# Output product of an attention kernel as seven block products instead of eight

## The chip, the cores and the metric

The kernel runs on one core of one Trainium2 chip. The metric is its device time in microseconds: median 2259.83 us of three runs (2258.32 to 2260.1).

## What is computed

Three steps on 4 sequences of 512 tokens, each 1024 wide, all in fp32: a gated feed-forward step, latent attention with 32 heads, and the feed-forward step again, each added to x. The change is in the attention:

```python
q = rms_norm(x @ wq_a.T, q_norm_w) @ wq_b.T            # 32 heads: 128 plain, 64 rotated columns
kv_up = rms_norm(kv_c, kv_norm_w) @ wkv_b.T            # keys and values from 128 latents
scores = (q_nope . k_nope + q_pe . k_pe) * scale       # causal
probs = softmax(scores)
out = (probs . v).reshape(b, s, 32 * 128)
x = x + out @ wo.T                                     # [512, 4096] x [4096, 1024] per sequence
```

## The kernel before

An fp32 number is kept as two fp32r parts, high and low, and a product is three matmuls: high x high, high x low, low x high (`three`, L781; `products` issues them, the matmul is L777).

Attention treats two of the four sequences at a time (a pair, p = 0 and 1) and two heads at a time (a group, g = 0 to 15). A group has four slots, k = 0 to 3; a slot is half of one sequence for both heads. Slots of even k take the first half and have few keys ("even slots"), those of odd k the second half ("odd slots"). In slot k PE does, by an order written out in `slot` (L1191): the four score tiles of the slot (`scores`), the transposes of the four probability tiles of the slot before (`turn_probs`), the values of the slot before (`values`), the output product of the slot before that (`output`), and "fills", which prepare queries and weights and are spread over the slots by the table `FILLS`: q0 to q3 and pe0, pe1 (nine matmuls 512 columns wide each), and in pair 0 also m0 to m3 (value weights times output weights, one true fp32 matmul 512 wide) and w0, w1.

The values of a slot are [latent 128] x [2 heads x 256 rows]. The output product multiplies them with `w_out` (2 heads x 1024 columns): four outputs of 128 rows x 512 columns, j = 0 to 3, each six matmuls (two heads x three), which is eight block products of three matmuls. The bank of output j is one of two (`bank_y`), so PE waits for the addition of output j-2 to `xacc`.

- ACT reads PSUM and writes high parts (`hi`, L1303): `turned` for transposes, `valued` for values, `read_fill`; it also does the exponentials (`exps`, L1579).
- DVE does masks and maxima (`maxima`), the low parts (`lo`, L1692: `pt_split`, `o_split`, fills), the scaling of probabilities (`norms`, L2029) and the additions (`y_add`, L2041).
- POOL does the rotation of the rotated query half, five links of 512 columns (`rotate`, L2278 to L2286), twice a group, after a swap by DMA, and the low part of the rotated weights (`split_wpe`, L2257).
- SP issues the swaps and stacks of the rotation, loads of weights, and in pair 0 stores `w_out` (`keep_wo`); in pair 1 ACT issues its reload (`out_weights`).

Each engine goes through its list in order. `settle` is a semaphore increment between waits.

## Time and profile before

| | |
|---|---|
| median of the runs | 2259.83 us |
| span of the profiled execution | 2257.3 us |
| PE busy | 2213.3 us, 98% |
| DVE busy | 1594.8 us, 71% |
| ACT busy | 968.0 us, 43% |
| POOL busy | 576.2 us, 26% |
| steady group in pair 0 (4 slots) | 63.10 us |
| steady group in pair 1 (4 slots) | 57.57 us |

No time of the profiled execution beyond its span is shown; the median lies 2.5 us above the span. The two attention stages repeat exactly from group to group, so one group is read closely and multiplied.

### The profile page before, as it was taken

What the parts mean: (1) busy time and instruction counts of PE and PEld (TensorE: products, weight loads), DVE (VectorE), ACT (ScalarE), POOL (GpSimd) and SP (SyncE); (2) the same over time, 40 slices, a digit from 0 to 9 for tenths busy, and PEclk for the clock granted to TensorE, in tenths of its full rate; (3) what the DMA queues carried; (4) which work ended last, traced back from release to release, by engine and by line L of the source; (5) the groups of instructions that cost most, each with busy time, mean ns of one, the idle gap of its engine ahead of it and who ended that gap; (6) DMA issues with size and microseconds to landing.
All of it is one profiled execution on the core that took longest, in us unless ns stands there. A gap on an engine that the chain in (4) does not pass through costs nothing.

```text
span 2257.3 us, 39455 instructions
## 1 busy us (share of the span) xinstructions
PE 2213.3 (98%) x11932; PEld 1871.3 (83%) x11932; DVE 1594.8 (71%) x3663; ACT 968.0 (43%) x2441; POOL 576.2 (26%) x642
## 2 busy tenths in 40 slices
PE   8989999999999999999999999999999999999998
PEld 7978888888888888887788988888888888888887
DVE  7656667776676766777787666766777766666777
ACT  6543444443444443443465534334344443334344
POOL 5312222122221222212144332222222222222212
PEclk9999999999999999999999999999999999999999
DMA  4023333332233333333423123333323333333321
GB/s 161 15 72 114 113 113 103 113 86 87 76 103 110 111 113 112 104 108 105 154 86 98 44 77 83 82 82 82 81 80 81 82 82 82 82 82 82 79 71 75
DMA packets 217433, 207.09 MB, mean 92 GB/s; under 512 B 144288, under 2 KB 172832, under 8 KB 215328
## 3 DMA queue, kind: packets, MB, share of 16 engines
q1 hardware_dynamic: 196928, 162.32, 25.7%
q10 hardware_dynamic: 20448, 44.04, 5.8%
q8 instruction: 32, 0.52, 0.1%
q14 instruction: 25, 0.20, 0.0%
HBM read 101.45 MB, written 54.53 MB: 69 GB/s over the span
## 4 chain that ended last, share of the span: by engine, by line
PE 88%; DVE 5%; issue 2%; DMA 2%; ACT 1%; POOL 1%; SPq 0%; ACTq 0%; DVEq 0%; POOLq 0%
PE ps L777 69%; PE ps L1141 6%; PE ps L856 4%; PE ps L1085 2%; PE ps L791 1%; PE ps L803 1%; DVE stage L2029 1%; DVE arena L1692 1%; PE ps L1092 1%; PE ps L1123 1%; ACT arena L1303 1%; DVE negmax L2019 1%; PE ps L805 1%; PE ps L1119 1%; DVE stats L1701 0%
## 5 line engine op out<-in xcount | busy, mean ns | idle before, releaser
L777 PE MATMUL ps<-arena 128*128 128x512 f32 x3264 | 876.9, 404 | 8.9 <-DVE xacc L1794 4.9
L1692 DVE TENSOR_TENSOR arena<-ps,arena 128x512 fp32r<-128x512 f32 (+2 forms) x920 | 538.4, 597 | 414.2 <-ACT arena L1303 414.0
L1303 ACT ACTIVATE arena<-ps 128x512 fp32r<-128x512 f32 (+2 forms) x920 | 471.8, 525 | 656.8 <-PE ps L777 429.6
L777 PEld LDWEIGHTS ps<-arena 128*128 128x128 f32 x3264 | 578.2, 188 | 119.6 <-issue 10.0
L777 PE MATMUL ps<-zT,arena 128*128 128x512 f32 (+1 forms) x1746 | 438.9, 395 | 1.7 <-DVE ropeT L1692 0.8
L1579 ACT ACTIVATE stage<-ps,negmax 128x128 f32<-128x128 f32 (+6 forms) x512 | 259.9, 508 | 368.3 <-DVE negmax L2019 360.6
L2041 DVE TENSOR_TENSOR xacc<-ps,xacc 128x512 f32<-128x512 f32 x512 | 350.0, 684 | 64.9 <-PE ps L777 58.3
L777 PEld LDWEIGHTS ps<-zT,arena 128*128 128x128 f32 x1746 | 320.2, 188 | 75.9 <-issue 5.6
L2278 POOL TENSOR_TENSOR stage<-stage,pos_tab 128x512 f32<-128x512 f32 (+1 forms) x66 | 83.3, 1262 | 973.7 <-ACT stage L1303 951.9
L777 PE MATMUL ps<-keyT,arena 128*128 128x192 f32 (+5 forms) x1152 | 267.7, 341 | 4.8 <-ACT stage L1579 4.6
L2019 DVE TENSOR_REDUCE negmax<-ps 128x1 f32<-128x128 f32 (+6 forms) x512 | 238.6, 466 | 17.6
L777 PE MATMUL ps<-arena,lat 128*128 128x512 f32 (+1 forms) x1152 | 245.6, 357 | 0.3 <-issue 0.2
L777 PEld LDWEIGHTS ps<-arena,lat 128*128 128x128 f32 x1152 | 204.4, 188 | 48.6 <-issue 7.9
L777 PEld LDWEIGHTS ps<-keyT,arena 128*128 128x128 f32 x1152 | 198.1, 189 | 53.7 <-issue 15.5
L1141 PE MATMUL ps<-ident,stage 128*128 128x128 f32 (+1 forms) x1280 | 202.4, 273 | 1.7 <-DVE arena L1692 0.9
L777 PE MATMUL ps<-ropeT,arena 128*128 128x192 f32 (+5 forms) x768 | 189.2, 327 | 0.0
L2029 DVE TENSOR_SCALAR stage<-stage,rrec 128x128 f32<-128x128 f32 (+6 forms) x512 | 180.0, 415 | 4.8 <-DVE rrec L2025 0.3
L1141 PEld LDWEIGHTS ps<-ident,stage 128*128 128x128 f32 (+1 forms) x1280 | 151.1, 136 | 29.4 <-issue 9.2
L2017 DVE TENSOR_TENSOR ps<-ps,mask 128x64 f32<-128x64 f32 (+1 forms) x512 | 120.9, 236 | 44.8 <-PE ps L777 30.5
L777 PEld LDWEIGHTS ps<-ropeT,arena 128*128 128x128 f32 x768 | 132.0, 189 | 7.5
L2283 POOL TENSOR_TENSOR stage<-stage,pos_tab 128x512 f32<-128x512 f32 (+1 forms) x66 | 83.2, 1261 | 174.1 <-DMA stage<-stage 174.1
L1303 ACT ACTIVATE stage<-ps 128x512 f32<-128x512 f32 (+3 forms) x130 | 63.7, 495 | 111.6 <-PE ps L777 67.9
(103 smaller groups left out, 1853.0 us busy)
## 6 DMA issues: line engine op xcount, KB each, us to landing
kept_out<-arena SPq DMA_DIRECT2D x16, 2048.0 KB, 6.4
arena<-arena SPq DMA_DIRECT2D x248, 128.0 KB, 3.0
arena<-kept_out ACTq DMA_DIRECT2D x30, 1024.0 KB, 5.9
stage<-in_wo SPq DMA_DIRECT2D x16, 1024.0 KB, 6.0
stage<-stage SPq DMA_DIRECT2D x248, 64.0 KB, 2.0
kept_q<-arena SPq DMA_DIRECT2D x16, 768.0 KB, 7.5
arena<-kept_q ACTq DMA_DIRECT2D x32, 384.0 KB, 3.4
out<-xacc SPq DMA_DIRECT2D x15, 512.0 KB, 2.7
```

The source lines that it names most:

```text
L777: last = nc.tensor.matmul(dst, w, m, start=start and n == 0, stop=stop and n == len(passes) - 1, skip_group_check=skip)
L856: last = nc.tensor.matmul(bzs[half], xnT[:, b, xp, k * P:(k + 1) * P], w_lat[:, wp, k, half * ZH:(half + 1) * ZH], start=(k == 0 and c == ...
L1141: last = nc.tensor.transpose(turned_at(u, i)[0:w, j * P:(j + 1) * P], prob[u][:, poff(u, i) + j * P:poff(u, i) + j * P + w], ident[:, :])
L1303: return nc.scalar.activation(dst, src, ACT.Copy)
L1579: nc.scalar.activation(prob[u][:, poff(u, i):poff(u, i) + w], bank_s(i)[:, 0:w], ACT.Exp, bias=negmax[:, k % 2, i:i + 1], accum_out=rowsum ...
L1692: return nc.vector.tensor_tensor(dst, src, part.bitcast(F32), ALU.subtract)
L2017: nc.vector.tensor_tensor(diagonal, diagonal, masks, ALU.add).then_inc(masked, 1)
L2019: nc.vector.tensor_reduce(negmax[:, u, i:i + 1], bank_s(i)[:, 0:keys_of(u, i)], AX_X, ALU.max, negate=True).then_inc(max_ready, 1)
L2029: nc.vector.tensor_scalar(pr, pr, rrec[:, u, i:i + 1], None, ALU.mult).then_inc(prob_ready, 1)
L2041: nc.vector.tensor_tensor(xs, bank_y(j), xs, ALU.add).then_inc(y_added, 1)
L2278: link(G.tensor_tensor(both, raw, pos_tab[:, 0, c0:c1], ALU.mult))
L2283: link(G.tensor_tensor(swapped, swapped, pos_tab[:, 1, c0:c1], ALU.mult))
```

## The change

The values of a slot are a 2 x 2 matrix of blocks (row halves x heads), and the output weights are 2 x 2 blocks (heads x column halves). The eight block products become seven, by a form of Strassen's identity: seven left operands, `a11, a12, s2, s1, s3, a22, s4`, four of them sums, and seven right operands, `B11, B21, T2, T1, T3, T4, B22`, again four of them sums. Each product is three matmuls of 512 columns and writes one of two banks; four of the products accumulate onto what their bank holds (`Y_NEW` lists those that start it), and after every product the bank is added to a place of `xacc` (`Y_INTO`), so that some sums reach two places. The seven are spread over the slot one at a time.

The left sums are made on POOL in every slot (`sums`: four subtractions of 128 columns, three low parts of 256, 256 and 384), from plain values that ACT writes in two pieces (`valued`); ACT writes three high parts (`split_a`). The low part that DVE made of the values (`o_split`) goes. The right sums are made once a group, in pair 0: the m fills are read plain into the staging buffer; POOL makes the four sums (`sum_b`, 512 columns each) and their low parts (`split_t`), ACT seven high parts and DVE three low parts (`split_b`). SP stores the seven operands (3584 KB a group instead of 2048 KB) and loads them back in pair 1 in seven pieces instead of two. The fills are spread anew; pe1 and pe0 stand earlier in their even slots. The norms of DVE stand before the addition of product 4. To make room, small tables share a buffer and are loaded again for pair 1.

The diff, cut to its core:

```diff
+NPROD = 7
+WB = NPROD * 2 * HALF
+w_prod = arena(0, NPROD, 2, HALF)
+w_plain = arena_plain(0, NPROD, 2, HALF)
...
+GAP = [PT0 + part * NS * SEQ + (NS - 1) * SEQ for part in range(2)]
+AT = {"s3": 0, "a22": 1, "s4": 2, "s1": 3, "s2": 4}
+GROUPS = [("a11", 2), ("s1", 2), ("s3", 3)]
+def operand(name, part, count=1, plain=False):
+    if name in AT:
+        return (extra_plain if plain else extra)(part * AE + AT[name] * P, count * P)
+    return (arena_plain if plain else arena)(GAP[part] + (P if name == "a12" else 0), count * P)
...
 FILLS = [{
-    "front":  [None, None, "m2", None],
-    "output": [None, "q3", "m3", "w1"],
-    "second": [None, "m0", "pe0", "q0"],
-    "first":  ["pe1", None, None, None],
-    "third":  ["q2", None, "w0", "q1"],
-    "values": [None, "m1", None, None],
+    "front":  [None, "m3", None, None],
+    "output": ["pe1", "q2", "pe0", "q0"],
+    "second": ["m0", "m1", None, "w1"],
+    "first":  ["m2", "q3", "w0", "q1"],
 }] + [{
-    "second": [None, "q2", None, "q0"],
-    "first":  ["pe1", None, "pe0", None],
-    "third":  [None, "q3", None, "q1"],
+    "output": ["pe1", "q2", "pe0", "q0"],
+    "first":  [None, "q3", None, "q1"],
 }] * (NPAIR - 1)
...
+Y_OPS = ["a11", "a12", "s2", "s1", "s3", "a22", "s4"]
+Y_NEW = [0, 1, 3]
+Y_INTO = [(0, 0), (0, 0), (1, 0), (1, 1), (1, 1), (1, 0), (0, 1)]
+B11, B21, T2, T1, T3, T4, B22 = range(NPROD)
+B_ORDER = [B11, B21, T1, T2, T3, T4, B22]
+def raw_at(name):
+    return s_wo[:, int(name[1]) % 2, int(name[1]) // 2 * HALF:(int(name[1]) // 2 + 1) * HALF]
+RAW = {B11: "m0", B21: "m1", B22: "m3"}
...
+    def keep_b(g):
+        sp.wait_ge(b_lo, 3 * g + 3)
         settle(sp)
-        sp.dma_start(kept_out[bass.ds(g, 1)].rearrange("a p h s n -> p (a h) s n"),
-                     w_out.bitcast(F32)).then_inc(wo_kept, 16)
+        sp.wait_ge(t_lo, 4 * g + 4)
+        settle(sp)
+        sp.dma_start(kept_b[bass.ds(g, 1)].rearrange("a p n -> p (a n)"),
+                     arena(0, WB).bitcast(F32)).then_inc(wo_kept, 16)
+    def kept(g):
         sp.wait_ge(wo_kept, 16 * (g + 1))
         settle(sp)
+    def b_again(g, j):
+        s = slice(j * 2 * HALF, (j + 1) * 2 * HALF)
+        sp.dma_start(arena(0, WB)[:, s].bitcast(F32),
+                     kept_b[bass.ds(g, 1), :, s].rearrange("a p n -> p (a n)")).then_inc(b_back[j], 16)
...
-    def output(p, g, k, j, first, last):
-        half = j // 2
+    def output(p, g, k, j, first):
         n = y_n(p, g, k) + j
-        if k == 2 and j % 2 == 0:
-            if p == 0:
-                a, d = weights_filled(last, first, half)
-                pe.wait_ge(q_act, qbase(p, g) + a)
-                pe.wait_ge(q_dve, qbase_d(p, g) + d)
+        if k == 2:
+            if p:
+                pe.wait_ge(b_back[j], 16 * (g + 1))
+            elif j in RAW:
+                pe.wait_ge(b_lo, 3 * g + list(RAW).index(j) + 1)
             else:
-                pe.wait_ge(o_back[half], 16 * (g + 1))
-        if j == 0:
-            pe.wait_ge(o_hi, slot_n(p, g, k) - 1)
-            pe.wait_ge(o_lo, slot_n(p, g, k) - 1)
+                pe.wait_ge(t_lo, 4 * g + [T1, T2, T3, T4].index(j) + 1)
+        if j % 2 == 0 and j < 6:
+            pe.wait_ge(o_lo, 3 * unit_n(p, g, k) + j // 2 + 1)
         if not (first and k == 2 and j < 2):
             pe.wait_ge(y_added, n - 1)
-        ts = slice(j % 2 * P, (j % 2 + 1) * P)
-        hs = slice(half * HALF, (half + 1) * HALF)
-        passes = []
-        for h in range(2):
-            passes += three(oT[:, k % 2, 0, h, ts], oT[:, k % 2, 1, h, ts], w_out[:, h, 0, hs], w_out[:, h, 1, hs])
-        products(bank_y(j), passes).then_inc(y_done, 1)
+        a = [operand(Y_OPS[j], part) for part in range(2)]
+        products(bank_y(k, j), three(a[0], a[1], w_prod[:, j, 0], w_prod[:, j, 1]),
+                 start=j in Y_NEW, skip=True).then_inc(y_done, 1)
...
     def slot(p, g, k, last=False):
         n, before = slot_n(p, g, k) - 1, (k - 1) % 4
         ev = q_events(p, last)
+        def out_(*js):
+            for j in js:
+                output(p, g, k, j, False)
         scores(p, g, k, 0, False, last)
         scores(p, g, k, 1, False, last)
         fills(p, g, k, "front", ev)
         turn_probs(n, before, 0, False)
         turn_probs(n, before, 1, False)
-        output(p, g, k, 0, False, last)
         fills(p, g, k, "output", ev)
         scores(p, g, k, 2, False, last)
+        out_(0)
         turn_probs(n, before, 2, False)
-        output(p, g, k, 1, False, last)
+        out_(1)
         fills(p, g, k, "second", ev)
+        out_(2)
         scores(p, g, k, 3, False, last)
+        out_(3)
         turn_probs(n, before, 3, False)
+        out_(4)
         fills(p, g, k, "first", ev)
-        output(p, g, k, 2, False, last)
-        fills(p, g, k, "third", ev)
+        out_(5)
         values(n, before, False)
-        fills(p, g, k, "values", ev)
-        output(p, g, k, 3, False, last)
+        out_(6)
...
+    def valued(n, used=0):
         act.wait_ge(pv_done, n + 1)
-        hi(oT[:, k % 2, 0].rearrange("p h (t s) -> p h t s", s=HQ), by_head(bank_pv)).then_inc(o_hi, 1)
+        if used:
+            act.wait_ge(y_done, used)
+        for a, name in enumerate(("a11", "s3")):
+            hi(operand(name, 1, 2, True).rearrange("p (h t s) -> p h t s", h=2, s=HQ),
+               by_head(bank_pv[:, a * 2 * P:(a + 1) * 2 * P])).then_inc(o_raw, 1)
+        split_a(n, 0)
+    def split_a(n, group):
+        if group:
+            act.wait_ge(o_sum, 4 * n + 2 * group)
+        else:
+            act.wait_ge(o_raw, 2 * n + 2)
+        name, count = GROUPS[group]
+        hi(operand(name, 0, count), operand(name, 1, count, True)).then_inc(o_hi, 1)
...
+            m = unit_n(p, g, k)
             apart(p, g, k)
             fills(k, "front")
             if k % 2 == 0:
                 turned(n, before, 0)
-            exps(p, g, k, 0)
-            if k % 2:
+                exps(p, g, k, 0)
+                turned(n, before, 1)
+                split_a(m, 1)
                 exps(p, g, k, 1)
+                split_a(m, 2)
+            else:
+                exps(p, g, k, 0)
                 turned(n, before, 0)
-            turned(n, before, 1)
-            if k % 2 == 0:
                 exps(p, g, k, 1)
+                turned(n, before, 1)
+                split_a(m, 1)
+                split_a(m, 2)
+            if k == 2 and p == 0:
+                split_b(g, T3, last)
+                split_b(g, T4, last)
             fills(k, "output")
+            if k == 1 and not last:
+                split_wpe(p, g + 1)
             turned(n, before, 2)
             exps(p, g, k, 2)
+            if k == 2 and p == 0:
+                freed(g, B22)
+                split_b(g, B22, last)
             fills(k, "second")
-            if k == 1 and p > 0:
-                out_weights(p, g, 0)
+            if k == 1 and p == 0:
+                freed(g, B11)
+                split_b(g, B11, last)
+                freed(g, B21)
+                split_b(g, B21, last)
+            exps(p, g, k, 3)
             turned(n, before, 3)
-            exps(p, g, k, 3)
+            if k == 1 and p == 0:
+                split_b(g, T1, last)
+                split_b(g, T2, last)
             fills(k, "first")
-            if k == 1 and not last:
-                split_wpe(p, g + 1)
-            fills(k, "third")
             if k == 1 and p > 0 and not last:
                 q_weights_back(g + 1, 0)
                 q_weights_back(g + 1, 1)
-            valued(n, before)
-            fills(k, "values")
-            if k == 1 and p > 0:
-                out_weights(p, g, 1)
+            valued(n)
...
-        y_add(p, g, k, 0)
         fills("output")
         maxima(p, g, k, 2)
+        adds(0)
         pt_split(n, before, 2)
-        y_add(p, g, k, 1)
+        adds(1)
         fills("second")
+        adds(2)
+        if k == 2 and p == 0:
+            split_b(g, B22)
         maxima(p, g, k, 3)
+        adds(3)
         pt_split(n, before, 3)
-        fills("first")
+        norms(p, g, k)
+        adds(4)
         if early:
             mom_early(g, k)
-        norms(p, g, k)
-        y_add(p, g, k, 2)
-        fills("third")
-        o_split(n, before)
-        fills("values")
-        y_add(p, g, k, 3)
+        fills("first")
+        adds(5)
+        if k == 1 and p == 0:
+            split_b(g, B11)
+            split_b(g, B21)
+        adds(6)
...
+    def sums(m, used=None):
+        a11, a12, a21, a22 = (operand(name, 1, 1, True) for name in ("a11", "a12", "s3", "a22"))
+        s1, s2, s3, s4 = (operand(name, 1, 1, True) for name in ("s1", "s2", "s3", "s4"))
+        def split(group):
+            pool.wait_ge(o_hi, 3 * m + group + 1)
+            settle(pool)
+            name, count = GROUPS[group]
+            G.tensor_tensor(operand(name, 1, count), operand(name, 1, count, True),
+                            operand(name, 0, count).bitcast(F32), ALU.subtract).then_inc(o_lo, 1)
+        pool.wait_ge(o_raw, 2 * m + 2)
+        settle(pool)
+        G.tensor_tensor(s1, a21, a11, ALU.subtract).then_inc(o_sum, 1)
+        pool.wait_ge(o_sum, 4 * m + 1)
+        settle(pool)
+        G.tensor_tensor(s2, a22, s1, ALU.subtract).then_inc(o_sum, 1)
+        pool.wait_ge(o_sum, 4 * m + 2)
+        settle(pool)
+        if used is not None:
+            pool.wait_ge(y_done, used)
+            settle(pool)
+        G.tensor_tensor(s4, a12, s2, ALU.subtract).then_inc(o_sum, 1)
+        pool.wait_ge(o_sum, 4 * m + 3)
+        settle(pool)
+        split(0)
+        G.tensor_tensor(s3, a22, a21, ALU.subtract).then_inc(o_sum, 1)
+        split(1)
+        split(2)
...
+    def sum_b(g, j, names, last):
+        t = [w_plain[:, T, 1] for T in (T1, T2, T3, T4)]
+        raw = [raw_at(name) for name in ("m0", "m1", "m2", "m3")]
+        pool.wait_ge(q_act, raw_filled(g, last, False, *names))
+        settle(pool)
+        pool.wait_ge(y_done, y_n(0, g, 1) + [T1, T2, T3, T4][j] + 1)
+        settle(pool)
+        if j == 0:
+            ins = G.tensor_tensor(t[0], raw[2], raw[3], ALU.add)
+        elif j == 1:
+            pool.wait_ge(t_sum, 4 * g + 1)
+            settle(pool)
+            ins = G.tensor_tensor(t[1], t[0], raw[0], ALU.subtract)
+        elif j == 2:
+            ins = G.tensor_tensor(t[2], raw[0], raw[2], ALU.subtract)
         else:
-            rotate(turns(p, g, 1), qbase(p, g) + ev["pe1"][0] + 1)
-        if not last and not first:
+            pool.wait_ge(t_sum, 4 * g + 2)
+            settle(pool)
+            ins = G.tensor_tensor(t[3], raw[1], t[1], ALU.subtract)
+        ins.then_inc(t_sum, 1)
+    def split_t(g, j):
+        pool.wait_ge(b_hi, NPROD * g + B_ORDER.index(j) + 1)
+        settle(pool)
+        G.tensor_tensor(w_prod[:, j, 1], w_plain[:, j, 1], w_prod[:, j, 0].bitcast(F32),
+                        ALU.subtract).then_inc(t_lo, 1)
...
+    def body(p, g, last=False):
+        ev = q_events(p, last)
+        sums(unit_n(p, g, 0), y_n(p, g, 0))
+        rotate(turns(p, g, 1), qbase(p, g) + ev["pe1"][0] + 1)
+        sums(unit_n(p, g, 1), y_n(p, g, 1))
+        if not last:
             split_wpe(p, g + 1)
+        if p == 0:
+            sum_b(g, 0, ("m2", "m3"), last)
+            sum_b(g, 1, ("m0",), last)
+            split_t(g, T1)
+            sum_b(g, 2, ("m0", "m2"), last)
+            sum_b(g, 3, ("m1",), last)
+            split_t(g, T2)
+        sums(unit_n(p, g, 2), y_n(p, g, 2))
+        if p == 0:
+            split_t(g, T3)
+            split_t(g, T4)
         if not last:
-            rotate(turns(p, g, 1) + 1 + first, qbase(p, g) + ev["pe0"][0] + 1)
+            rotate(turns(p, g, 1) + 1, qbase(p, g) + ev["pe0"][0] + 1)
+        sums(unit_n(p, g, 3), y_n(p, g, 3))
```

## Rows read from the trace of the kernel before

**Rows 1.** The page's first part: busy time, share of the span, instructions.
```profile
PE 2213.3 (98%) x11932; PEld 1871.3 (83%) x11932; DVE 1594.8 (71%) x3663; ACT 968.0 (43%) x2441; POOL 576.2 (26%) x642
PEclk9999999999999999999999999999999999999999
```

**Rows 2.** Windows of one group of pair 0 and one of pair 1: busy us.
```profile
core 0: us, PE busy (x) PEld busy (x) DVE busy (x) ACT busy (x) POOL busy (x), PEclk, DMA share, GB/s
885.98:949.08 63.10, 62.64 (x319) 51.56 (x319) 43.91 (x103) 26.12 (x69) 14.15 (x11) 1.00 0.34 101
1371.62:1429.19 57.57, 57.55 (x300) 48.72 (x299) 40.32 (x97) 22.99 (x63) 14.16 (x11) 1.00 0.31 81
```

**Rows 3.** Timeline, PE, an even slot of pair 1: start us, us, operation.
```profile
1393.98 0.28 PE L1119 MATMUL ps<-keyT,arena 128*128 128x256 f32 x1
1394.68 0.82 PE L1141 MATMUL ps<-ident,stage 128*128 128x128 f32 x6
...
1405.97 1.55 PE L777 MATMUL ps<-arena 128*128 128x512 f32 x6
1407.36 0.60 PE L777 MATMUL ps<-keyT,arena 128*128 128x320 f32 x3
```

**Rows 4.** The page's groups of output and feed-forward matmuls and of additions.
```profile
L777 PE MATMUL ps<-arena 128*128 128x512 f32 x3264 | 876.9, 404 | 8.9 <-DVE xacc L1794 4.9
L2041 DVE TENSOR_TENSOR xacc<-ps,xacc 128x512 f32<-128x512 f32 x512 | 350.0, 684 | 64.9 <-PE ps L777 58.3
```

**Rows 5.** Groups by shape of POOL: busy us, mean ns of one, idle before.
```profile
L2278 POOL TENSOR_TENSOR stage<-stage,pos_tab 128x512 f32<-128x512 f32 x62 | 80.4, 1296 | 958.3 <-ACT stage L1303 951.3 <-issue 7.1
L2205 POOL TENSOR_TENSOR stage<-stage 128x136 f32<-128x136 f32 x32 | 15.4, 482 | 16.8 <-ACT stage L1303 16.5
L2286 POOL TENSOR_TENSOR arena<-stage,arena 128x256 fp32r<-128x256 f32 x4 | 3.0, 739 | 0.7 <-POOL stage L2285 0.7
L2257 POOL TENSOR_TENSOR arena<-stage,arena 128x384 fp32r<-128x384 f32 x32 | 38.6, 1206 | 219.9 <-ACT arena L1303 219.9
```

**Rows 6.** Timeline, POOL, the first links of one rotation in pair 1.
```profile
1374.71 1.29 POOL L2278 TENSOR_TENSOR stage<-stage,pos_tab 128x512 f32<-128x512 f32 x1 [11.96 <-ACT stage L1303]
1379.23 1.29 POOL L2283 TENSOR_TENSOR stage<-stage,pos_tab 128x512 f32<-128x512 f32 x1 [3.23 <-DMA stage<-stage]
1380.70 1.30 POOL L2284 TENSOR_TENSOR arena<-stage 128x512 fp32r<-128x512 f32 x1 [0.18 <-POOL stage L2283]
```

**Rows 7.** Timeline, DVE and ACT, the same even slot as rows 3.
```profile
1397.98 0.68 DVE L2041 TENSOR_TENSOR xacc<-ps,xacc 128x512 f32<-128x512 f32 x1
1398.45 0.59 ACT L1303 ACTIVATE arena<-ps 128x512 fp32r<-128x512 f32 x1
1398.58 0.22 DVE L2017 TENSOR_TENSOR ps<-ps,mask 128x64 f32<-128x64 f32 x1
1399.11 0.68 DVE L1692 TENSOR_TENSOR arena<-ps,arena 128x512 fp32r<-128x512 f32 x1
1401.02 0.47 ACT L1579 ACTIVATE stage<-ps,negmax 128x256 f32<-128x256 f32 x1
1401.83 0.98 DVE L2029 TENSOR_SCALAR stage<-stage,rrec 128x128 f32<-128x128 f32 x4
```

**Rows 8.** Timeline, DVE norms of two odd slots, and POOL beside the second.
```profile
1390.10 1.47 DVE L2029 TENSOR_SCALAR stage<-stage,rrec 128x320 f32<-128x320 f32 x4
907.51 2.22 DVE L2029 TENSOR_SCALAR stage<-stage,rrec 128x320 f32<-128x320 f32 x4
907.86 1.23 POOL L2257 TENSOR_TENSOR arena<-stage,arena 128x384 fp32r<-128x384 f32 x1 [9.24 <-ACT arena L1303]
```

**Rows 9.** Timeline, PE, a fill m2 of pair 0 and what follows it.
```profile
911.58 1.13 PE L1085 MATMUL ps<-stage 128*128 128x512 f32 x2 [0.46 <-DVE arena L1692]
912.54 0.82 PE L1141 MATMUL ps<-ident,stage 128*128 128x128 f32 x6
```

**Rows 10.** The page's DMA issues: KB each, median us to landing.
```profile
kept_out<-arena SPq DMA_DIRECT2D x16, 2048.0 KB, 6.4
stage<-in_wo SPq DMA_DIRECT2D x16, 1024.0 KB, 6.0
```

454 lines of the change are left out of this document (258 added, 196 removed).

## The prediction

> **What bounds the kernel now.** I read the page first: PE is busy 98% of the span at the full granted clock, 2.4 GHz, and no other engine passes 71% [rows 1]. Then the windows of one steady group of each pair. In pair 1 PE is busy 57.55 of 57.57 us, in pair 0 62.64 of 63.10 us; DVE is at 70%, ACT at 41%, POOL at 14.2 us [rows 2]. So the time is the sum of PE's instructions, and the other engines have idle time, though each must deliver in order. Then the timeline of PE, for what one matmul takes: six output matmuls stand between the starts 1405.97 and 1407.36, 1.39 us, 0.232 us each [rows 3]; the mean of 404 ns in the group row is the life of one and not the spacing [rows 4]. An even slot of pair 1 runs from 1393.98 to 1407.36, 13.38 us [rows 3]; an odd one takes the rest of half a group, 57.57/2 - 13.38 = 15.40 us.
>
> **What is removed from PE.** Eight block products of three matmuls become seven. Three matmuls less in each of 128 slots (16 groups x 4 x 2 pairs) are 384, at 0.232 us 89.3 us. Check of the count: 3264 matmuls in the row are 128 x 24 and 192 of the feed-forward step [rows 4]. The Trainium skill (TensorE: Matmul & The Clock Gate, Back-to-back issue gap) gives 131 ns sustained for 512 columns; by it the saving would be 50 us and the sum below 39 us higher, but the trace shows 232 ns. A new product has a wait of its own; before, a boundary between two kinds of work costs nothing beyond the spacing that one can see, so I charge none unless the wait is late. If nothing else mattered, an even slot of pair 1 would take 12.68 us, an odd one 14.70, the group 54.8; in pair 0 60.3.
>
> **What is added beside PE.** DVE: three more additions a slot at 0.68 us [rows 4], 0.60 when they follow each other (1397.98 to 1398.58 [rows 7]), minus one low part of 512 columns of about the same cost. About +1.2 us a slot; in pair 1 its busy time grows from 40.3 us a group [rows 2] to 45 of 54.8. That fits as a sum, but the order is fixed. ACT: the values in two pieces and three high parts; they are 128 to 384 columns wide, 512 take 0.59 [rows 7]; I take 0.4 each, so +1.4 us a slot with the old one gone, between 0.5 and 2.4. POOL: a link of 512 columns takes 1.29 us, of 256 0.74, of 136 0.48 [rows 5], and 0.18 passes between links [rows 6]. So the chain up to the first low part (three subtractions of 128 at 0.45, one of 256 at 0.74, and gaps) takes 2.7 us, and the whole of `sums` some 5.5 us. POOL rises from 14.2 us a group to about 36 in pair 1 and, with four sums and four low parts of 512 columns, 8 x 1.47 = 11.8 us, to about 48 of 60 in pair 0. Bounds for the links of 384: 1.0 by the slope of the others and 1.21 as measured.
>
> **Pair 1, even slot**, in us from PE's first score. Scores and two transposes end at 1.3, the pe fill that now stands there (9 x 0.232 = 2.09) at 3.4, score 2 at 3.9. Product 0 ends at 4.6, transpose 2 at 5.0, products 1 and 2 at 6.4, score 3 at 7.0, product 3 at 7.7, transpose 3 at 8.05, products 4 and 5 at 9.45, values at 11.95, product 6 at 12.65.
> - ACT reads the pe fill and two more high parts ahead of transpose 2: it reaches the transpose at about 5.4 instead of 5.15 and ends at 6.0 (0.59 [rows 7]). DVE then makes the low part, and addition 1 ends at 7.3. Product 3 needs that bank at 7.0: 0.35 us.
> - Additions 1 and 2 stand ahead of maximum 3: it ends at 8.4. Exponential 0.47, transpose 3 read in 0.6, low part 0.68 [rows 7], each behind the other: 10.3 us. Before, a pe fill of 2.1 us and an output of 1.4 us lay between the transpose and the values; now only products 4 and 5. The values are wanted at 9.45 + 0.35: 0.5 us.
> - The norms start at 10.3. The rotation, whose fill is read at 5.5, gets its swapped half 4 to 4.5 us later (1374.71 to 1379.23 [rows 6]) and then runs four links, from 9.5 to 15.3. So norms and rotation meet in every even slot. What that costs is shown where POOL's split of 384 columns runs beside the norms: four norms take 2.22 us instead of 1.47 [rows 8], for one POOL instruction. With links following each other I expect them to wait for the end of two, so +1.4 us on 0.98 [rows 7]; the bounds are 0.5 and 3. Addition 4 then ends at 13.3, and product 6, which needs its bank, is wanted at 12.8: 0.5 us.
>
> The Trainium skill (SBUF — State Buffer, Who interferes with whom) says that VectorE in a two-port mode and GpSimd exclude each other for a whole instruction; [rows 8] agree, and this rule speaks against the change.
>
> Sum of an even slot 1.35 us. **Odd slot:** POOL is busy with the rotation until 1.2 us into it. ACT's last high part waits for POOL's last sum, and the q fill is read behind it, 5.0 to 5.6; DVE does its low part, maximum 2 and only then addition 0, until 7.7; product 2 wants the bank at 6.6. That is 1.1 us, 0.6 if POOL were in time; I take 0.85. Both slots twice: 4.4 us a group, against 2.8 gained.
>
> **Pair 0.** m fills of 0.93 us (911.58 to 912.54 [rows 9]) stand between products and cover most of what was counted above in slots 0 and 1 (0.2 us left). Slot 1 takes 15.40 - 0.70 + 2 x 0.93 = 16.5 us. POOL may make the first right sum when product 3 of slot 1 is through, at 11.1. Then four sums and two low parts, 6 x 1.47 = 8.8, until 19.9, and only then the left sums of slot 2, 2.7 us: at 22.6, or 6.1 into slot 2, where PE wants them at 3.9: 2.2 us. The last left sum is later still, and ACT waits for it and makes two high parts before it reads the pe fill and transpose 2: I count 1.9 us more at product 3 and at the values and product 6. The rotation then runs into slot 3: 0.5 us at product 2 there. Sum 4.8 us a group, against 2.8 gained. The store of 3584 KB at the rate of 2048 KB in 6.4 us [rows 10] is 11.2 us; the next load of output weights is behind it and wanted 5.7 us into the next group. It fits by about a microsecond; without that cover PE waits up to 2 us a group (not in the sum, in the range). The reload in pair 1 is issued a slot ahead and hidden.
>
> **Sum**, against the span of 2257.3: -89.3, +15 x 4.8 = 72 (steady groups of pair 0), +15 x 4.4 = 66 (pair 1), +2 for first and last slots: +51, 2308. The median of the runs lies 2.5 us above the span: 2310 us.
>
> **Rivals.**
> - A, the covers hold in pair 1: ACT and DVE deliver earlier than I laid out, and the second chain above is late by less than the gain. For: DVE's idle time of 30% [rows 2]. Against: the chain exponential, transpose, low part is short of cover by half a microsecond at best. With no wait in pair 1: 2310 - 66 = 2244; with one us a group 2259.
> - B, POOL is in time as well, and the saving shows whole: 2259.8 - 89 + 2 = 2173. Against: the six links behind product 3 of slot 1, whose durations rows give. It would take links half as long.
> - C, worse on the slow side: norms and POOL alternate one for one, so that each even slot waits one link more, 60 x 1.47 = 88 us: 2398. It decides if DVE gets one norm and not two into each gap of POOL.
> - D, the change doesn't do what it says: the new products start with a gap on PE (a wait read late), 0.23 us each in 896 products would cost 206 us and give over 2370.
>
> **How the numbers follow.** Forecast 0.52 (2270 to 2350; 0.02 of it within 0.2%). A 0.26 (0.20 faster, 0.05 same, 0.01 slower). B 0.09. C 0.10, D 0.03. Faster by over 0.2%: 0.20 + 0.09 = 0.29; within 0.2%, or 4.5 us, about what a measurement of this kernel can tell: 0.07; slower 0.64. The range is 2225 to 2350: it leaves out B and most of C and D, and takes in A and the bounds of the norms (0.9 us less to 1.6 more in 60 slots, of which PE sees half).
>
> **What would show it.** PE's busy share falls from 98%; matmuls of the output row fall by 384. In the windows a group of pair 1 takes 58 to 60 us and one of pair 0 64 to 66; PE's waits name DVE's additions (`xacc`) and low parts (`arena`), in pair 0 also POOL. The norms' mean rises in even slots only. Groups of 55 and 60 us would show me wrong; so would waits of PE below 3 us a group.

## The result, and the profile after

The changed kernel takes 2415.36 us (median of 4, 2413.81 to 2419.02) beside 2259.97 us of the kernel before: a ratio of 1.0689 (95% interval 1.0674 to 1.0704). The forecast was slower, 2310 us, range 2225 to 2350: the sign held, the size did not. The profiled spans differ by 2417.4 - 2257.3 = 160.1 us where 51 were worked out.

From the page: span and busy time ([rows 1] before), PE's clock, the dearest groups ([rows 4] before), the store of the right operands ([rows 10] before).

```profile
span 2417.4 us, 44695 instructions
PE 2221.8 (92%) x11548; PEld 1830.0 (76%) x11548; DVE 1881.5 (78%) x3912; ACT 1154.0 (48%) x3065; POOL 1279.9 (53%) x1658
PEclk9989999999999999999999989999999999999999
...
L835 PE MATMUL ps<-arena,extra 128*128 128x512 f32 x1920 | 593.6, 422 | 113.1 <-DVE xacc L2154 109.3
L2154 DVE TENSOR_TENSOR xacc<-ps,xacc 128x512 f32<-128x512 f32 x896 | 602.3, 682 | 66.5 <-PE ps L835 56.8
...
L2139 DVE TENSOR_SCALAR stage<-stage,rrec 128x128 f32<-128x128 f32 (+6 forms) x512 | 297.1, 641 | 4.5
...
kept_b<-arena SPq DMA_DIRECT2D x16, 3584.0 KB, 11.0
```

384 matmuls are gone (11932 to 11548, [rows 1]), and PE stands still 8% of the span. It waits 109.3 us for DVE's additions (L2154), since the bank of a product is not yet added. The additions are no longer than before (682 ns, 684 in [rows 4]); the norms (L2139) are: 641 ns in the mean, 415 in the kernel before (L2029, 512 of them). So DVE comes late. POOL's busy time has doubled and more.

Windows of one group of pair 0 and one of pair 1 (columns as in [rows 2]):

```profile
878.36:946.89 68.53, 62.96 (x308) 50.82 (x306) 55.08 (x109) 33.57 (x93) 42.04 (x47) 0.98 0.36 116
1992.89:2053.09 60.20, 56.80 (x287) 46.30 (x286) 47.30 (x104) 27.03 (x80) 30.81 (x39) 1.00 0.36 103
```

They were 63.10 and 57.57 us [rows 2]; forecast were 65.1 and 59.2. The table gives slots, as means over 13 steady groups of pair 0 and 14 of pair 1, from PE's first score of one slot to that of the next. "Ideal" is the kernel before with 0.70 us less in each slot.

| kernel | median | slot 0 | slot 1 | slot 2 | slot 3 | pair 0 | even | odd | pair 1 |
|---|---|---|---|---|---|---|---|---|---|
| before | 2259.97 | 15.51 | 15.07 | 16.58 | 15.93 | 63.1 | 13.53 | 15.26 | 57.6 |
| ideal | 2170.7 | 14.8 | 14.4 | 15.9 | 15.2 | 60.3 | 12.8 | 14.6 | 54.8 |
| before_less | 2208.25 | 15.00 | 14.37 | 16.60 | 15.24 | 61.2 | 12.83 | 14.99 | 55.6 |
| before_pool | 2277.52 | 15.50 | 15.07 | 17.63 | 15.92 | 64.1 | 13.53 | 15.26 | 57.6 |
| **after** | 2415.36 | 14.82 | 20.70 | 17.91 | 15.25 | 68.7 | 14.27 | 15.86 | 60.3 |
| norm_one_port | 2407.61 | 14.63 | 17.51 | 19.13 | 15.74 | 67.0 | 13.84 | 16.77 | 61.2 |
| norm_act | 2414.60 | 14.64 | 18.43 | 19.29 | 15.62 | 68.0 | 13.86 | 16.66 | 61.1 |
| right_narrow | 2353.04 | 14.95 | 17.03 | 17.37 | 15.25 | 64.6 | 14.28 | 15.86 | 60.3 |
| adds_narrow | 2398.68 | 14.76 | 20.28 | 16.55 | 16.08 | 67.7 | 13.73 | 16.45 | 60.4 |
| act_order | 2394.20 | 15.07 | 20.78 | 17.91 | 15.24 | 69.0 | 14.17 | 15.02 | 58.4 |
| mix1 | 2394.79 | 14.90 | 18.43 | 18.61 | 16.41 | 68.4 | 13.82 | 15.39 | 58.4 |
| mix2 | 2360.43 | 15.09 | 17.51 | 19.16 | 15.24 | 67.0 | 14.18 | 15.02 | 58.4 |
| order_narrow | 2320.30 | 14.93 | 17.03 | 16.56 | 15.24 | 63.8 | 14.16 | 15.02 | 58.4 |
| order_rot | 2378.03 | 15.05 | 20.84 | 17.92 | 15.24 | 69.1 | 13.74 | 15.03 | 57.5 |
| order_norm | 2382.71 | 14.97 | 20.78 | 17.90 | 15.24 | 68.9 | 13.81 | 15.02 | 57.7 |
| bound | 2300.19 | 14.94 | 17.04 | 16.66 | 15.24 | 63.9 | 13.74 | 15.03 | 57.5 |

Slot 1 of pair 0 stands out: 20.70 us, forecast 16.7 (the 16.5 of the prediction and its 0.2 for small waits). Timeline of its end, DVE, POOL, PE:

```profile
906.75 5.32 DVE L2139 TENSOR_SCALAR stage<-stage,rrec 128x320 f32<-128x320 f32 x4
911.99 0.68 DVE L2154 TENSOR_TENSOR xacc<-ps,xacc 128x512 f32<-128x512 f32 x1
...
906.45 1.28 POOL L2470 TENSOR_TENSOR arena_plain<-arena_plain,stage 128x512 f32<-128x512 f32 x1 [0.18 <-POOL arena_plain L2466]
907.69 1.37 POOL L2482 TENSOR_TENSOR arena<-arena_plain,arena 128x512 fp32r<-128x512 f32 x1
909.03 1.38 POOL L2472 TENSOR_TENSOR arena_plain<-stage 128x512 f32<-128x512 f32 x1
910.37 1.41 POOL L2476 TENSOR_TENSOR arena_plain<-stage,arena_plain 128x512 f32<-128x512 f32 x1
911.74 1.45 POOL L2482 TENSOR_TENSOR arena<-arena_plain,arena 128x512 fp32r<-128x512 f32 x1
...
912.72 0.96 PE L835 MATMUL ps<-arena,extra 128*128 128x512 f32 x3 [3.17 <-DVE xacc L2154]
```

The four norms take 5.32 us; alone they take 1.47 [rows 8]. The surplus, 3.85 us, is three of POOL's instructions: as they follow each other with no gap, one norm gets through at each boundary. Looked at one by one, the norms end at 907.92, 909.28, 910.66 and 912.06 us, each 0.2 to 0.3 us after one of POOL's instructions. It is the same in every steady group (5.30 to 5.32 us). The addition of product 4 stands behind the norms, and PE waits 3.17 us for it with product 6.

In pair 1 the same meeting is the one that was forecast (even slot, DVE, POOL, PE; last row the odd slot):

```profile
2033.39 2.38 DVE L2139 TENSOR_SCALAR stage<-stage,rrec 128x128 f32<-128x128 f32 x4
...
2034.11 1.29 POOL L2422 TENSOR_TENSOR arena<-stage 128x512 fp32r<-128x512 f32 x1 [0.18 <-POOL stage L2421]
...
2033.52 2.68 PE L835 MATMUL ps<-arena,lat 128*128 128x512 f32 x12 [0.41 <-DVE arena L1801]
2036.43 0.98 PE L835 MATMUL ps<-arena,extra 128*128 128x512 f32 x3 [0.24 <-DVE xacc L2154]
2044.97 0.96 PE L835 MATMUL ps<-arena,extra 128*128 128x512 f32 x3 [1.01 <-DVE xacc L2154]
```

### The profile page after: what moved, and what is told of

Same layout as the page of the kernel before. It is cut to its first block, busy times and chain, and to the rows that moved or that the text cites. A ratio compares the mean times of both kernels' runs of the same rounds, so it can differ in the third digit from the quotient of the medians.

```text
span 2417.4 us, 44695 instructions
## 1 busy us (share of the span) xinstructions
PE 2221.8 (92%) x11548; PEld 1830.0 (76%) x11548; DVE 1881.5 (78%) x3912; ACT 1154.0 (48%) x3065; POOL 1279.9 (53%) x1658
## 4 chain that ended last, share of the span: by engine, by line
PE 49%; DVE 22%; ACT 11%; issue 10%; DMA 3%; POOL 3%; SPq 1%; DVEq 0%; ACTq 0%; POOLq 0%
PE ps L835 37%; DVE stage L2139 6%; DVE xacc L2154 5%; ACT arena L1356 5%; PE ps L914 4%; DVE negmax L2129 3%; ACT stage L1653 3%; DVE arena L1801 3%; PE ps L1194 2%; DVE ps L2127 2%; PE ps L1138 2%; ACT extra L1356 1%; ACT stage L1356 1%; DVE ps L2120 1%; PE ps L861 1%
## 5 line engine op out<-in xcount | busy, mean ns | idle before, releaser
L835 PE MATMUL ps<-arena,extra 128*128 128x512 f32 x1920 | 593.6, 422 | 113.1 <-DVE xacc L2154 109.3
L2154 DVE TENSOR_TENSOR xacc<-ps,xacc 128x512 f32<-128x512 f32 x896 | 602.3, 682 | 66.5 <-PE ps L835 56.8
L1801 DVE TENSOR_TENSOR arena<-ps,arena 128x512 fp32r<-128x512 f32 (+4 forms) x728 | 417.5, 575 | 299.3 <-ACT arena L1356 298.8
L835 PEld LDWEIGHTS ps<-arena,extra 128*128 128x128 f32 x1920 | 332.5, 190 | 227.8 <-DVE xacc L2154 154.1
L1356 ACT ACTIVATE arena<-ps 128x512 fp32r<-128x512 f32 (+4 forms) x728 | 363.4, 503 | 180.4 <-PE ps L835 88.3
L2439 POOL TENSOR_TENSOR extra_plain<-extra_plain,arena_plain 128x128 f32<-128x128 f32 x128 | 59.2, 463 | 467.4 <-ACT extra_plain L1356 467.4
L2139 DVE TENSOR_SCALAR stage<-stage,rrec 128x128 f32<-128x128 f32 (+6 forms) x512 | 297.1, 641 | 4.5
L835 PE MATMUL ps<-arena 128*128 128x512 f32 x960 | 282.5, 412 | 8.8 <-DVE xacc L1903 4.9
L2435 POOL TENSOR_TENSOR extra<-extra_plain,extra 128x256 fp32r<-128x256 f32 (+1 forms) x256 | 222.8, 875 | 98.8 <-ACT extra L1356 97.3
L835 PE MATMUL ps<-arena,lat 128*128 128x512 f32 (+1 forms) x1152 | 248.6, 360 | 17.9 <-DVE arena L1801 17.2
L835 PEld LDWEIGHTS ps<-arena 128*128 128x128 f32 x960 | 166.6, 192 | 31.6 <-DVE xacc L1903 6.9
```

The costliest lines, as they stand in the source:

```text
L835: last = nc.tensor.matmul(dst, w, m, start=start and n == 0, stop=stop and n == len(passes) - 1, skip_group_check=skip)
L1356: return nc.scalar.activation(dst, src, ACT.Copy)
L1801: return nc.vector.tensor_tensor(dst, src, part.bitcast(F32), ALU.subtract)
L2139: nc.vector.tensor_scalar(pr, pr, rrec[:, u, i:i + 1], None, ALU.mult).then_inc(prob_ready, 1)
L2154: nc.vector.tensor_tensor(xs, bank_y(k, j), xs, ALU.add).then_inc(y_added, 1)
L2435: G.tensor_tensor(operand(name, 1, count), operand(name, 1, count, True), operand(name, 0, count).bitcast(F32), ALU.subtract).then_inc(o_l ...
```

## The experiments

Each kernel below ran on the same chip as the kernel before, which took 2261.3, 2258.8, 2259.6 and 2259.4 us on the four chips used. Ratios are to that. "After" was not run again on them, so a gain against after is the difference of two such comparisons, with an uncertainty of some 5 us.

**What was there to be had: before_less.**

```diff
-                    passes += three(oT[:, k % 2, 0, h, ts], ...)
+                    if j < 3 or h == 0:
+                        passes += three(oT[:, k % 2, 0, h, ts], ...)
```

> The kernel before with three matmuls fewer in every slot: the second head is left out of output 3, so part of the output product is missing, and nothing else is changed. It measures the saving by itself. Theory: 384 matmuls at 0.232 us are the whole effect, 2260 - 89 = 2171 us. Rival: another engine binds as soon as PE is shorter, and less than half of that comes out, above 2215 us.

Measured 2208.25 us, ratio 0.9765 (0.9745 to 0.9784): 53 us, not 89, so neither number came: more than half of the saving comes out, and not all of it. PE's waits in this kernel:

```profile
PE ps L1085 <- DVE arena L1693: 16.7, 14, 1.6
PE ps L1119 <- DMA arena<-arena: 9.5, 15, 1.0
```

Taken off PE alone, with nothing added anywhere, the matmuls uncover two chains that had been just in time: a fill's low part in slot 2 of pair 0 (7.0 us in the kernel before, 14 times) and the stack of the rotated half at the start of even slots of pair 1 (none there before). Slot 2 does not get shorter at all. The two waits have grown by 19 us together; the other 17 us of the 36 that are missing are not traced.

**The price of POOL beside norms, by itself: before_pool** (the kernel before, steady groups of pair 0).

```diff
                     split_wpe(p, g + 1)
+                    if p == 0:
+                        for i in range(6):
+                            G.tensor_tensor(hw[...], pos_tab[:, 0], pos_tab[:, 1], ALU.mult)
```

Each of the six waits for the one before it.

> The kernel before with nothing of the change but six more links of POOL, 512 columns wide, in slot 1 of each of 14 steady groups of pair 0, right behind the low part that lay beside the norms there; they write a buffer that nobody reads. Theory, norms and back to back links hinder each other: the four norms of slot 1, 2.22 us beside one POOL instruction, grow to 5 us or more (5.32 in the kernel after), and since everything behind them on DVE is in order, slot 1 of pair 0 grows by 1 to 3 us; 14 groups, 2275 to 2300 us. Rival, the norms of the kernel after were long for another reason (a wait inside them that is not POOL's): they stay near 2.2 us and the time stays at 2260. If they grow and the time does not, the price of the kernel after comes only with its narrower covers.

Measured 2277.52 us, 1.0076 (1.0059 to 1.0092). DVE and POOL at the end of slot 1, PE at the start of slot 2:

```profile
921.62 3.27 DVE L2030 TENSOR_SCALAR stage<-stage,rrec 128x320 f32<-128x320 f32 x4
...
921.96 1.22 POOL L2258 TENSOR_TENSOR arena<-stage,arena 128x384 fp32r<-128x384 f32 x1 [9.24 <-ACT arena L1304]
923.15 1.46 POOL L2300 TENSOR_TENSOR hw<-pos_tab 128x512 f32<-128x512 f32 x1
924.78 1.28 POOL L2300 TENSOR_TENSOR hw<-pos_tab 128x512 f32<-128x512 f32 x1 [0.18 <-POOL hw L2300]
...
926.74 1.12 PE L1086 MATMUL ps<-stage 128*128 128x512 f32 x2 [1.51 <-DVE arena L1693]
```

The norms grow from 2.22 [rows 8] to 3.27 us, by one POOL instruction more beside them; the others come after. PE's wait for the fill grows from 0.46 [rows 9] to 1.51 us: the whole 1.05 us arrives on PE, in the kernel that has all its matmuls. In all that is 14 us in 13 steady groups; the group after them grows by 3.7 us. The number I expected for the norms (5 us) was wrong, since they began before the links did, and it is slot 2 that grows (16.58 to 17.63 us) and not slot 1; the mechanism and the time held.

**Norms that don't meet POOL: norm_one_port and norm_act.** The first adds an accumulator output to each norm; the second has ACT do them.

```diff
-nc.vector.tensor_scalar(pr, pr, rrec[...], None, ALU.mult)
+nc.vector.tensor_scalar(pr, pr, rrec[...], 0.0, ALU.mult, ALU.add, accum_out=normsum[...])
```

> The changed kernel (2415 us); only the form of DVE's four norms is another one, tensor_scalar with an accumulator written out. Theory (norms and POOL wait for each other for the port): the four norms of slot 1 of pair 0 fall from 5.3 us to under 3, in even slots from 2.4 to 1.5, although the form may itself be slower; PE's wait of 3.2 us at product 6 of that slot goes, a group of pair 0 falls from 68.5 to about 65, one of pair 1 from 60.25 to about 59.5: 2350 us. Rival (the three more additions and the longer chains of DVE and ACT are the cost, wherever the norms stand): within 20 us of 2415, since the order and the number of instructions are the same.

Measured 2407.61 us, 1.0648 (1.0630 to 1.0666). First and last norm of slot 1 beside the same POOL instructions:

```profile
890.13 0.55 DVE L2140 TENSOR_SCALAR_CACHE_REDUCE stage<-stage,rrec 128x320 f32<-128x320 f32 x1
...
891.74 0.74 DVE L2140 TENSOR_SCALAR_CACHE_REDUCE stage<-stage,rrec 128x512 f32<-128x512 f32 x1
```

Four norms in 892.48 - 890.13 = 2.35 us instead of 5.32, and none is held. The Trainium skill (SBUF — State Buffer, Who interferes with whom) excepts just this form from those that take the ports shared with GpSimd; the trace agrees. Slot 1 falls by 3.2 us, even slots of pair 1 by 0.43. But slot 2 rises by 1.2 and odd slots by 0.9, and the total is the rival's, within 20 us of 2415. One cause is that the form is slower (742 ns at 512 columns in the mean, 478 for the plain form in the kernel before). In slot 2 there is a second: the meeting with POOL has moved. Two low parts of the right operands (`split_b`: B11, B21), both of whose inputs lie in SBUF, now stand beside POOL's unbroken instructions. Here they are, norm_one_port and then after:

```profile
894.20 2.91 DVE L1802 TENSOR_TENSOR arena<-stage,arena 128x512 fp32r<-128x512 f32 x2
```

```profile
913.78 1.54 DVE L1801 TENSOR_TENSOR arena<-stage,arena 128x512 fp32r<-128x512 f32 x2
```

One alone takes 0.67 us. The masks and maxima of slot 2 stand behind them, and PE waits 1.47 us for an exponential at score 2.

norm_act drops the norms from DVE's list and adds, behind `turned(n, before, 3)` of each slot:

```diff
+for i in range(NS):
+    nc.scalar.activation(pr, pr, ACT.Copy, scale=rrec[:, u, i:i + 1]).then_inc(prob_ready, 1)
```

> The changed kernel (2415 us) with the four norms of a slot moved from DVE to ACT (which multiplies by the same reciprocals, after it has read transpose 3); DVE keeps the reciprocal. Nothing that uses the port stands in the norms' place any more, and the slower form of norm_one_port isn't needed. Theory (port): slot 1 of pair 0 falls from 20.4 to below 17, even slots of pair 1 from 14.26 to 13.8, odd ones stay at or below 15.86 instead of the 16.75 of norm_one_port; 2330 to 2345 us. Rival (the order of the chain sets the period of two slots whatever the norms do, as adds_narrow left the pair of slots at 30.12 us): slot 1 of pair 0 gains, pair 1 stays at 60.2, 2360 to 2370 us.

Measured 2414.60 us, 1.0687 (1.0669 to 1.0705): slot 1 falls by 2.3 us, slot 2 rises by 1.4, odd slots by 0.8, and the time is above both numbers. PE waits 24.7 us for POOL's left low parts and 26.5 for exponentials. ACT has more to do before it gives these out; and here too the two low parts of the right operands are held, 1.0 and 1.77 us instead of 0.67. Which of the two costs slot 2 its 1.4 us was not tried apart.

**POOL's right sums: right_narrow.**

```diff
-t = [w_plain[:, T, 1] for T in (T1, T2, T3, T4)]
+t = [w_plain[:, T, 1, 0:8] for T in (T1, T2, T3, T4)]
```

The low parts are cut to 8 columns likewise, and ACT makes its high parts in the steady groups from the block m0, since the sums aren't there.

> The changed kernel; in the steady groups POOL's four right sums and four low parts are 8 columns wide instead of 512 (so the right operands of pair 0 are not those of the reference), and all waits stay. Theory: slot 1 of pair 0 falls from 20.4 to 17 us, because the norms find POOL free, and slot 2 from 18.1 to about 15.5, because POOL reaches its left sums in time; group 68.5 to about 62.5, pair 1 stays at 60.25: 2325 us. Rival (POOL's right sums run beside other delays): less than 30 us gained.

Measured 2353.04 us, 1.0404 (1.0387 to 1.0421), 62 us less than after. It lies between the two numbers. The norms of slot 1 take 1.48 us in every steady group. Slot 1 falls by 3.7 us, slot 2 by 0.5 and not by the 2.2 us that I had laid to POOL's lateness there: something else holds slot 2 at 17.4.

**DVE's additions: adds_narrow** (products 1, 2 and 4).

```diff
+if j in (1, 2, 4):
+    xs, ys = xs[:, 0:8], ys[:, 0:8]
```

> The changed kernel; the additions of products 1, 2 and 4 are 8 columns wide (their products are missing in the output but for 8 columns), so DVE has four full additions a slot as before the change. Theory (an addition costs time where it stands ahead of maximum 3 or of product 6): even slots of pair 1 fall from 14.26 to about 13.2, odd ones from 15.86 to 15.4, group of pair 1 to 57.2, pair 0 to about 66: 2335 us. Rival (only norms against POOL matter): under 25 us gained.

Measured 2398.68 us, 1.0610 (1.0592 to 1.0628). The even slot falls by 0.54 us and the odd one rises by 0.59; the total is the rival's, under 25 us gained. DVE's busy time is not the bound of pair 1: with less of it two slots still take 30.2 us (30.1 in after). That points to a chain that spans both slots; the next kernel tests it.

**ACT's order: act_order.**

```diff
                 turned(n, before, 1)
-                split_a(m, 1)
                 exps(p, g, k, 1)
-                split_a(m, 2)
+                split_a(m, 1)
...
-                split_a(m, 2)
                 fills(k, "output")
                 turned(n, before, 2)
+                split_a(m, 2)
```

In slot 2 of pair 0 the high parts of T3 and T4 go behind the last line too.

> The changed kernel with another order on ACT alone: the pe or q fill and transpose 2 are read before the last high part of the left operands (and in slot 2 of pair 0 before the high parts of T3 and T4), so that they no longer wait behind POOL's last sum. Theory (a chain over two slots: pe fill read, swap by DMA, rotation, left sums, ACT's last high part, q fill read, low part, maximum 2, addition 0, product 2): odd slots of pair 1 fall from 15.86 to about 15.2, slot 2 of pair 0 from 18.1 to about 17; 2375 us. Rival (ACT's order is not on the path): within 10 us of 2415.

Measured 2394.20 us, 1.0599 (1.0579 to 1.0619), between the two numbers. Odd slots of pair 1 fall from 15.86 to 15.02 us, their wait before product 2 from 1.01 to 0.18 us. That is the chain of the period: ACT's last high part waited for POOL's last sum, and the fill's read behind it. Slot 2 of pair 0 did not move, against my number.

**First slots of pair 1: late_back and reload_narrow.** The first group of pair 1 took 51.1 us from its first score to that of the next group, and 62.0 after. In after (PE, then SP's issues):

```profile
1413.72 0.55 PE L1172 MATMUL ps<-keyT,arena 128*128 128x256 f32 x1 [3.21 <-DMA extra<-arena]
1421.96 4.18 PE L835 MATMUL ps<-zT,arena 128*128 128x512 f32 x9 [6.62 <-POOL arena L2395]
...
1397.68 4.41 SPq L613 DMA_DIRECT2D arena<-kept_b  x7
1402.22 3.67 SPq L730 DMA_DIRECT2D extra<-arena  x4
```

The seven reloads stand ahead of the stack that a score needs, and POOL's rotation and low part of weights behind that. The 9.2 us of the two expectations below are the time from issue to landing of the stack's last copy; PE waits 3.2 us for it.

```diff
-    for j in range(NPROD):
-        b_again(0, j)
...
     stack_halves(turns(p, 0, 1) + 1, 1, None, PART, SEQ)
+    if p > 0:
+        for j in range(NPROD):
+            b_again(0, j)
```

> The changed kernel; SP issues the seven first reloads of pair 1 (3584 KB) after the rotated halves of the first group and not ahead of them. Theory: the 9.2 us that the first score of slot 1 spends waiting for the rotated half is the queue behind the reloads; the first slots of pair 1 lose about 10 us and the rest stays: 2405 us. Rival (the half is late for POOL): under 2 us gained.

Measured 2420.83 us, 1.0714 (1.0696 to 1.0732): nothing gained, the rival's number. PE's waits for the stack and for POOL are shorter (none and 3.1 us), and a new one stands at the products:

```profile
1422.65 2.92 PE L835 MATMUL ps<-arena 128*128 128x512 f32 x6 [3.63 <-DMA arena<-kept_b]
```

reload_narrow moves 8 columns of each of these seven:

```diff
-b_again(0, j)
+c = slice(j * 2 * HALF, j * 2 * HALF + 8)
+sp.dma_start(arena(0, WB)[:, c], kept_b[0, :, c]).then_inc(b_back[j], 16)
```

> The first reload of the seven operands in pair 1 moves 8 columns of each instead of 1024; all later ones stay whole. Theory, the rotated half of the first group waits behind 3584 KB in the queues (9.2 us for a stack that takes 2.7 elsewhere), and late_back only moved the wait to the products themselves (3.6 us for the reload): without the bytes the first slots of pair 1 fall by 8 to 12 us, 2405 us. Rival, these slots wait for POOL's low part of the rotated weights and a rotation whatever is loaded: 2412 us or more.

Measured 2410.16 us, 1.0670 (1.0652 to 1.0688). In the whole time that is inside the uncertainty of the comparison with after; in the trace this group falls from 62.0 to 55.9 us. Without the bytes of the reload 6 of the 10.9 us are gone. Part of that is the clock, which was granted at 0.89 over this group in after and at 0.94 here (an estimate from these: 62.0 x 0.11 less 55.9 x 0.06, at most some 3 us).

**Together: mix1, mix2, order_narrow.** mix1 is norm_act, act_order and late_back; mix2 is act_order with the accumulator form in slot 1 of pair 0 alone; order_narrow is act_order with right_narrow.

```diff
-nc.vector.tensor_scalar(pr, pr, rrec[...], None, ALU.mult)
+if p == 0 and k == 1:
+    nc.vector.tensor_scalar(pr, pr, rrec[...], 0.0, ALU.mult, ALU.add, accum_out=normsum[...])
+else:
+    nc.vector.tensor_scalar(pr, pr, rrec[...], None, ALU.mult)
```

> norm_act, act_order and late_back together. If their causes are separate, the gains add up to 2275 to 2290 us; if the order and the norms act on the same chain, 2310 or more.

Measured 2394.79 us, 1.0604 (1.0586 to 1.0622): no better than act_order alone. The gains do not add.

> Whole computation. ACT's order as in the earlier run with that name, and the norms of slot 1 of pair 0 alone in the form with an accumulator, all others in their old form. Theory, the two causes add: that slot falls from 20.7 to 17.5 us as with the form everywhere, groups of pair 1 stay at 58.4, and 2394 - 16 x 3.2 = 2343 us. Rival, the longer norms (3.0 us instead of 1.5) pass their lateness on to slot 2, which grew by 1.2 us when the form was used everywhere: 2343 + 19 = 2362 us.

Measured 2360.43 us, 1.0457 (1.0438 to 1.0476): the rival's number. It is the fastest that computes the whole. Slot 1 is down to 17.51 us, and slot 2 rises to 19.16 with a new wait:

```profile
895.73 0.58 PE L836 MATMUL ps<-keyT,arena 128*128 128x192 f32 x3 [1.47 <-ACT stage L1654]
899.27 0.95 PE L836 MATMUL ps<-arena,extra 128*128 128x512 f32 x3 [0.58 <-POOL extra L2439]
```

PE enters slot 2 sooner, but exponentials and POOL's left low parts come no sooner. As in norm_one_port, the low parts of B11 and B21 are held by POOL on the way (1.22 and 1.77 us), and the maxima for these exponentials stand behind them.

> Leaves out most of the right sums (POOL makes 8 columns of each of the four sums and low parts) and has ACT's new order. Theory, in pair 0 the two are apart from each other: group 64.6 us in pair 0 and 58.4 in pair 1, 2353 - 21 = 2332 us, and slot 2 stays at 17.4, because its wait for the left sums is not POOL's lateness but the chain bank, addition, and high part of ACT. Rival, slot 2 was held by POOL and ACT together, and with both eased it falls to 16 or below: 2310 us or less.

Measured 2320.30 us, 1.0273 (1.0245 to 1.0300), between the two numbers: with POOL's right sums gone ACT's order pays in slot 2 too, 17.37 to 16.56 us. Slot 2 had been held by both.

**What pair 1 still loses: order_rot, order_norm, bound.**

```diff
-rotate(turns(p, g, 1), qbase(p, g) + ev["pe1"][0] + 1)
+rotate(turns(p, g, 1), qbase(p, g) + ev["pe1"][0] + 1, c1=8 if p else SEQ)
```

The rotation behind pe0 is cut likewise.

> With ACT's new order, and in pair 1 the links of POOL's rotation are 8 columns wide instead of 512 (the rotated queries of pair 1 are left out, all else whole). Theory, what pair 1 still loses comes from POOL: in the even slot the norms are no longer held, in the odd slot the left sums are in time. The even slot falls from 14.17 to 13.4 us, the odd one stays near 15.0 or falls to 14.8, a group takes 56.6 instead of 58.4 us, 2394 - 27 = 2367 us. Rival, the even slot loses at the chain exponential, transpose, low part, values (0.55 us) and at single products whose bank comes just in time (0.1 us each), and POOL only adds to an engine that has time: group 57.8 or more, 2385 us or more.

```diff
+if p and k % 2 == 0:
+    pr = pr[:, 0:8]
```

> With ACT's new order, and in pair 1 the norms of even slots scale 8 columns of each tile (most of the scaling is left out there). Against the run beside it this takes the norms away and leaves POOL as it is. Theory, norms held by POOL are the whole loss at product 6: even slot 14.17 to 13.7 us, the odd slot unchanged, group 57.4, 2380 us. Rival, the wait for the values goes with it or the odd slot falls too (POOL's links were held as well): group 56.8 or less, 2370 us.

Measured 2378.03 us, 1.0524 (1.0506 to 1.0541), and 2382.71 us, 1.0547 (1.0529 to 1.0565). Both free the even slot by about 0.4 us and leave the odd one. Norms of even slots, order_rot and then order_norm:

```profile
2035.69 0.98 DVE L2138 TENSOR_SCALAR stage<-stage,rrec 128x128 f32<-128x128 f32 x4
```

```profile
2038.03 1.94 DVE L2140 TENSOR_SCALAR stage<-stage,rrec 128x8 f32<-128x8 f32 x4
```

Without the rotation full norms take 0.98 us, as before [rows 7]; with it, norms of 8 columns take 1.94. Three of these four take 0.5 us at most, and one takes 1.29, as long as POOL's instruction beside it. What is paid is the wait for that instruction, not the work. order_norm is near its theory's group (57.7 us for 57.4), order_rot lies between theory and rival (57.5 for 56.6 and 57.8): in pair 1 the held norms cost 0.7 to 0.9 us a group. The other 2.7 us above the ideal 54.8 I put down to the chains of ACT and DVE; no run takes those apart.

bound is order_narrow with the edits of order_rot and reload_narrow.

> ACT's new order, POOL's right sums and low parts 8 columns wide, POOL's rotation in pair 1 8 columns wide, the first reload of pair 1 8 columns wide: nearly all that is new on POOL but the left sums is gone. Theory, the terms add: 2320 less 27 for the rotation and 5 for the reload, 2288 us, still slower than the kernel before, since the 8% of PE's work that was a cover is gone and DVE's and ACT's chains alone hold it. Rival, POOL was the only cause: 2230 us or less.

Measured 2300.19 us, 1.0182 (1.0165 to 1.0199). With POOL's right sums, the rotation of pair 1 and the first reload all but gone the kernel is still 41 us slower than before. It is near the theory's 2288 us. So with these orders on PE, ACT and DVE, moving or hiding that work on POOL would not make the change pay. The left sums are still on POOL, and other orders of ACT and DVE were not tried. That the chains lack the cover which the matmuls gave is what before_less suggests; here it is argued and not shown.

## Why the prediction was right in its sign and wrong in its size

**What was missed, in numbers.** A steady group of pair 0 takes 68.67 us and not 65.1: 15 x 3.6 = 54 us. One of pair 1 takes 60.26 and not 59.2: 15 x 1.1 = 16 us. The rest of the kernel was to fall by 4 us (two groups' saving less the 2 us charged) and rises by 36: 40 us. Together 110; the spans miss by 109.

**The step that failed**, for the largest part, is "The norms' mean rises in even slots only", and with it "Slot 1 takes 15.40 - 0.70 + 2 x 0.93 = 16.5 us". I laid out POOL's eight links of slot 1 only for when they end, as a delay of the left sums of slot 2. That they run through the norms of slot 1, and without the 0.18 us between links of a rotation, I did not ask, though the prediction gives both times: first sum at 11.1 us, and norms of an odd slot next to POOL dearer [rows 8]. Slot 1 is 4.0 us over its forecast, more than the whole miss of pair 0; slots 0 to 3 stand at 14.8, 20.7, 17.9, 15.25 against 15.1, 16.7, 17.4, 15.9 (the prediction's 65.1 us laid out by slots). norm_one_port and right_narrow take 3.2 and 3.7 us out of it, before_pool shows the mechanism in the kernel before.

**Rival C** said what decides, one norm and not two into each gap of POOL. That is what happens, at another place than it named: in slot 1 of pair 0 (surplus of three instructions) and not in even slots, where two go into a gap (2.38 us; forecast 0.98 + 1.4). Its 2398 us is near by accident.

**Slot 2 of pair 0**: 17.9 us against 17.4, the total is near by luck. The split was not right: POOL's late left sums were to cost 2.2 us of it, and right_narrow frees 0.5. Only with ACT's order mended as well does it fall, to 16.56.

**Pair 1, even slot**: 14.27 us against 14.03, and here the mechanism was right, term by term. PE in the even slot whose norms and waits the section on the result shows:

```profile
2026.98 0.88 PE L835 MATMUL ps<-arena 128*128 128x512 f32 x3
2027.70 0.60 PE L1194 MATMUL ps<-ident,stage 128*128 128x128 f32 x4
2028.06 0.94 PE L835 MATMUL ps<-arena 128*128 128x512 f32 x3
2028.84 0.86 PE L835 MATMUL ps<-arena,extra 128*128 128x512 f32 x3
...
2029.88 0.40 PE L835 MATMUL ps<-ropeT,extra 128*128 128x256 f32 x2
2030.32 0.97 PE L835 MATMUL ps<-arena,extra 128*128 128x512 f32 x3
2031.13 0.60 PE L1194 MATMUL ps<-ident,stage 128*128 128x128 f32 x4
2031.48 1.62 PE L835 MATMUL ps<-arena,extra 128*128 128x512 f32 x6
```

The idle time in brackets is shorter than the delay, since a matmul's row lasts 0.39 us where the next starts after 0.23. From start to start: the two matmuls before product 3 take 0.44 us, and 0.23 where the product behind them is not held (slot 0 of pair 0), so it is 0.2 us late (forecast 0.35). Products 4 and 5 need 0.78 and 0.70, the values start after 2.04: 0.56 late (0.5). Product 6 starts 2.91 us behind the values, which take 2.40 unheld (1403.57 to 1405.97 in the kernel before): 0.5 late (0.5). Work that had to wait also takes 0.1 us longer before the next can start: product 3 takes 2031.13 - 2030.32 = 0.81 us. The rest of the difference is the slot before the change: I took the shorter of the two even slots, 13.38 us; the other takes 13.68.

Product 0 takes 2027.70 - 2026.98 = 0.72 us, about three times 0.232, so rival D (0.23 us for each product) is out. Product 1 takes 0.78. That is no wait: it stands behind transposes, and an output of six matmuls behind transposes took 1.46 us in the kernel before where others took 1.39. So "a boundary costs nothing that one can see" was off by 0.07 us at such places, in both kernels alike.

**Odd slot**: 15.86 against 15.55. Before product 2 PE idles 1.01 us, 1.2 from start to start; forecast were 1.1, of which I took 0.85. act_order gives most of it back: the cause was as told. **Rival A** (covers hold in pair 1): out. **Rival B** (the saving shows whole): out already without any added work, for before_less loses 36 of the 89 us. I had put every loss down to what is added, so the first term of the sum, -89.3, was not to be had whole in this kernel; by the rate of 0.232 it is also 89.1. (The m fill, 0.93 us in the prediction, is 0.96 by its rows.)

**Store and reload.** The store lands in 11.0 us, as estimated (11.2). "The reload in pair 1 is issued a slot ahead and hidden" holds for steady groups and fails for the first: 6 us, some of it the clock.

**Outside steady groups** I charged 2 us by no row; this is the second step that failed, 40 of the 109 us. The rise of 36 is 2 us before the first slot, 8 in the first and the last two groups of pair 0, 9 from its last slot to the first score of pair 1 (the feed-forward step between the pairs), 11 in the first group of pair 1 and 6 at the end. The reload is up to 6 of these 11. Of the 9 us some 3 go with the clock. reload_narrow is the same kernel up to that point and had the full clock there (windows from PE's last slot of pair 0 to the first score of pair 1, after and then reload_narrow):

```profile
1209.60:1388.50 178.90, 167.22 (x1117) 151.53 (x1115) 133.04 (x262) 100.19 (x186) 79.71 (x162) 0.98 0.31 104
```

```profile
1210.00:1385.60 175.60, 163.97 (x1116) 148.60 (x1114) 133.63 (x262) 99.92 (x186) 79.79 (x162) 1.00 0.31 105
```

The kernel before takes 169.5 us there, at 1.00. The other 6 us, and the rest of the 36, stay open.

## What to carry to other kernels

Where PE is 98% busy, its work is also the cover of all chains: take the matmuls out alone first and see what is left of the saving (here 53 of 89 us), before adding work elsewhere. Lay an engine's new instructions against the other engines' timelines for what they hold up while they run, not only for when they end; here each of DVE's scalings of 320 to 512 columns paid one POOL instruction where POOL's work was unbroken, and cutting the scaling to 8 columns did not take the wait away where POOL had gaps. When the scalings took a form that isn't held, the next DVE instructions with both inputs in SBUF were held instead. When one cause is taken away and the slot next to it grows, the saving is in the next chain, and a sum of separate gains (mix1, mix2) was not to be had.

## What the runs showed of the hardware

The clock fell behind a wait. Windows over the first 6 us of slot 2 in two neighbouring groups of after, and the two groups whole:

```profile
844.00:850.00 6.00, 5.70 (x32) 4.55 (x33) 5.46 (x13) 2.19 (x7) 4.21 (x7) 1.00 0.00 0
913.00:919.00 6.00, 6.00 (x28) 5.03 (x28) 5.42 (x13) 2.19 (x7) 4.07 (x7) 0.72 0.00 0
...
809.31:878.36 69.05, 62.02 (x307) 49.32 (x306) 55.45 (x109) 33.57 (x93) 42.03 (x47) 1.00 0.36 115
878.36:946.89 68.53, 62.96 (x308) 50.82 (x306) 55.08 (x109) 33.57 (x93) 42.04 (x47) 0.98 0.36 116
```

Both stretches come behind the same wait of 3.17 us. In one the granted clock stays at 1.00, in the other it is 0.72, so for about half the stretch it is the lower level, 1.2 GHz instead of 2.4; a fill of nine matmuls takes 3.35 us there instead of 2.35:

```profile
915.47 3.35 PE L835 MATMUL ps<-zT,arena 128*128 128x512 f32 x9
```

```profile
846.36 2.35 PE L835 MATMUL ps<-zT,arena 128*128 128x512 f32 x9
854.82 0.96 PE L835 MATMUL ps<-arena,extra 128*128 128x512 f32 x3 [1.56 <-DVE xacc L2154]
```

And yet the group with the slow stretch is not longer (68.53 against 69.05 us), and slot 2 takes 18.1 us in both. PE at full clock only waits the more for DVE (1.56 us before product 3, 0.87 in the other). The other steady groups of pair 0 say the same: of the 13, the two at 1.00 take 69.10 and 69.05 us, the eleven at 0.95 to 0.98 take 68.35 to 69.17. So in pair 0 the drop is a follower of the waits and not a cause of the time; in the step between the pairs, where PE is busy 167 of 179 us, it costs the 3 us told above. Why one group has it and its neighbour has not, no run here tells.
